# One megabyte of expert weights loaded before the router's table exists, and stores waited for one use later

## The reference

```python
x = x + gnn0(layernorm(x))    # h = x W_conv; sum of messages over edges; h W_lin + b_lin
x = x + ffn0(layernorm(x))    # a small 3-layer network on decoded features of each row
x = x + gnn1(layernorm(x))    # 3 times: relu(A (x W[l]) + b[l]), W[l] is 512x512
x = x + ffn1(layernorm(x))    # a tree of 15 tests picks one of 16 experts for each row
# expert e: gelu(x W1[e] + b1[e]) W2[e] + b2[e],  W1[e] 512x2048, W2[e] 2048x512, float32
```

## Time and profile before

| | us |
|---|---|
| median of 3 runs | 576.83 (575.34 to 577.37) |
| the profiled execution, its time | 578.86 |
| its span, first to last instruction | 577.1 |
| PE busy | 526.0 (91%) |
| DVE busy | 188.4 (33%) |
| ACT busy | 143.6 (25%) |
| POOL busy | 73.1 (13%) |
| mean granted TensorE clock | 0.978 of full |

### The profile page before, as it was taken

One profiled execution on the slowest core, in us unless ns is written; L12 is line 12 of the kernel. 1 busy time (PEld: TensorE's weight loads), 2 busy tenths in 40 slices (PEclk: granted clock), 3 DMA queues, 4 the chain that ended last, 5 costly groups with the idle time before them and its releaser, 6 DMA issues.

```text
span 577.1 us, 10036 instructions
## 1 busy us (share of the span) xinstructions
PE 526.0 (91%) x3215; PEld 286.8 (50%) x3215; DVE 188.4 (33%) x566; ACT 143.6 (25%) x504; POOL 73.1 (13%) x99
## 2 busy tenths in 40 slices
PE   1969999989999999999999599999999999978884
PEld 1536667544457466445455245555544364434332
DVE  5998999644410110256730100111111011100110
ACT  1547666112102011003122112222222042202211
POOL 4000000090000000000002222211211212122011
PEclk9979999979999999999999799999999999999998
DMA  6159930001120010027799999999999999999980
GB/s 128 14 174 429 429 133 19 18 1 53 39 73 2 0 73 0 7 86 229 288 389 418 413 396 424 420 424 423 422 423 419 419 430 412 421 416 433 420 371 21
DMA packets 26513, 145.84 MB, mean 253 GB/s; under 512 B 10479, under 2 KB 12729, under 8 KB 16882
## 3 DMA queue, kind: packets, MB, share of 16 engines
q1 hardware_dynamic: 23282, 142.92, 61.4%
q0 software_dynamic: 3200, 2.50, 2.1%
HBM read 142.38 MB, written 4.72 MB: 255 GB/s over the span
## 4 chain that ended last, share of the span: by engine, by line
PE 68%; DMA 16%; DVE 8%; issue 3%; ACT 2%; DVEq 1%; ACTq 1%; POOL 0%; POOLq 0%; SPq 0%
PE P L1168 14%; PE P L1082 13%; DMA w<-in_L_ffn_W 12%; PE P L955 9%; PE P L965 7%; PE P L789 6%; PE P L974 4%; DMA XT<-normed_rows,C 2%; PE P L1133 2%; DMA out<-XT,C 2%; DVE stats L1317 2%; DVE H L1292 1%; PE P L790 1%; PE P L1146 1%; PE P L869 1%
## 5 line engine op out<-in xcount | busy, mean ns | idle before, releaser
L1168 PE MATMUL P<-w,FB 128*64 128x256 f32 x1024 | 115.9, 383 | 2.2 <-DMA w<-in_L_ffn_W 2.2
L1082 PE MATMUL P<-w,H 128*64 128x512 f32 x448 | 100.0, 595 | 9.3 <-DMA w<-in_L_ffn_W 8.8
L1168 PEld LDWEIGHTS P<-w,FB 128*64 128x64 f32 x1024 | 72.1, 138 | 40.6 <-issue 6.6
L718 ACT ACTIVATE FB<-P,FB 128x64 f32<-128x64 f32 x256 | 54.4, 361 | 121.8 <-PE P L1133 121.8
L1575 DVE COPY H<-P 128x512 f32<-128x512 f32 x30 | 20.7, 692 | 195.5 <-PE P L1082 195.0
L789 PE MATMUL P<-H 125*126 125x500 bf16 x176 | 59.0, 414 | 8.1 <-DVE H L1292 4.7
L1082 PEld LDWEIGHTS P<-w,H 128*64 128x64 f32 x448 | 32.1, 137 | 68.7 <-issue 59.3
L1292 DVE TENSOR_SCALAR H<-iota,small 125x626 bf16<-125x626 f16 x176 | 56.6, 382 | 8.7 <-issue 6.9
L619 ACT ACTIVATE H<-G,small 125x126 bf16<-125x126 f16 x132 | 44.2, 392 | 35.3 <-PE P L790 21.8
L955 PE MATMUL P<-G,XT 128*125 128x512 f32 x120 | 52.0, 592 | 0.0
L965 PE MATMUL P<-C,H 125*128 125x313 f32 (+1 forms) x160 | 42.4, 425 | 0.0
(11 more groups left out here) (315 smaller groups left out, 441.8 us busy)
## 6 DMA issues: line engine op xcount, KB each, us to landing
w<-in_L_ffn_W SPq DMA_DIRECT2D x53, 2048.0 KB, 24.8
w<-in_L_ffn_W SPq DMA_DIRECT2D x14, 1024.0 KB, 9.6
G<-in_L_gnn_W SPq DMA_DIRECT2D x3, 1024.0 KB, 5.3
G<-in_L_ffn_W SPq DMA_DIRECT2D x2, 1024.0 KB, 8.3
C<-in_L_ffn_W SPq DMA_DIRECT2D x2, 1024.0 KB, 9.4
xs<-in_L_ffn_W SPq DMA_DIRECT2D x2, 1024.0 KB, 10.2
xn<-in_L_ffn_W SPq DMA_DIRECT2D x2, 1024.0 KB, 10.3
xs<-in_x SPq DMA_DIRECT2D x1, 1120.0 KB
```

The lines of the kernel that those rows point to most:

```text
L718: g = nc.scalar.activation(hT[:, m, :], P[:, 3 + rd, c * SA:(c + 1) * SA], ACT.Gelu, bias=bT[b][:, m:m + 1])
L1082: mm = nc.tensor.matmul(P[g * SA:(g + 1) * SA, h, :], xT[b][:, k, :], w1a[k][:, h, g], start=(k == 0), stop=(k == KD - 1))
L1168: mm = nc.tensor.matmul(P[g * SA:(g + 1) * SA, 7, 0:256], hT[:, m, :], w2_sb[b][:, m, g * 256:(g + 1) * 256], start=False, stop=(m == MH - 1))
```

## The change

- SP: after the block of tile 2's W1 that goes to xs, it waits until the router's last logits are out (`s_lgT` is 2) and loads the first quarter of tile 2's W2 to `XT[:, 0:2048]`. The later load of that quarter to `w2_sb[0]` is gone. PE's second layer of tile 2 takes quarter 0 from there.
- The small arrays leave that part of XT: `y_sb` to the last chunk of xs, `x_row` and `x_rowB` to the last chunk of xn, `y_sbB` to H, `sel` to the end of XT. DVE therefore waits for the stored norm rows ahead of the copy to `x_row`, and clears `x_rowB` after it, no longer behind the one-hot; ACT waits for the stored rows of x.
- POOL: a store is waited for when its `y_sb` buffer is used again, two tiles later. `s_yfree` is raised in `scatter`, after the next gather is issued.
- POOL starts its part of the second norm once `feat` is written. PE does one more `keep_warm` matmul between the feature transposes and the first layer of `ffn0`.

```diff
--- before.py
+++ after.py
@@ -183,11 +183,13 @@
         xTB = H[:, 2048:2048 + KD * SB_].rearrange("p (k s) -> p k s", k=KD)
         hT = FB[:, 0:MH * SA].rearrange("p (m s) -> p m s", m=MH)
         hTB = FB[:, MH * SA:MH * ROWS].rearrange("p (m s) -> p m s", m=MH)
-        y_sb = [XT[:, 1024 + b * 256:1280 + b * 256] for b in range(2)]
-        y_sbB = XT[:, 384:512]
-        sel = XT[:, 1792:1792 + NCH * SA].rearrange("p (c s) -> p c s", c=NCH)
-        x_row = XT[:, 0:256]
-        x_rowB = XT[0:2 * SB_, 512:768]
+        y_sb = [xs[:, NCH - 1, b * 256:(b + 1) * 256] for b in range(2)]
+        y_sbB = H[:, 2176:2304]
+        sel = XT[:, 2048:2048 + NCH * SA].rearrange("p (c s) -> p c s", c=NCH)
+        x_row = xn[:, NCH - 1, 0:256]
+        x_rowB = xn[0:2 * SB_, NCH - 1, 256:512]
+
+        w2_two = XT[:, 0:HID].rearrange("p (m n) -> p m n", m=4)
 
 
         maps = C[:, :, :].rearrange("p c n -> p (c n)")[:, HID:NCH * NPAD]
@@ -233,6 +235,7 @@
         s_edges, s_x, s_wconv, s_blin, s_cols = (sem(n) for n in ("edges_in", "x_in", "wconv_in", "blin_in", "cols_in"))
         s_wlin, s_ffnw, s_win, s_gw, s_bg2 = (sem(n) for n in ("wlin_in", "ffnw_in", "win_in", "gnnw_in", "bg2_in"))
         s_w1 = [[sem(f"w1_in{b}_{j}") for j in range(2)] for b in range(2)]
+        s_w2_two = sem("w2_in_tile2_quarter")
         s_w1_two, s_w2_end, s_w1q = sem("w1_in_tiles2_5"), sem("w2_in_end"), sem("tile0_w1_block_used")
         s_w2 = [[sem(f"w2_in{b}_{h}") for h in range(2)] for b in range(2)]
         s_iota, s_ident, s_rev, s_ones, s_loops, s_winz = (sem(n) for n in
@@ -374,6 +377,8 @@
             first_of_two(1)
             sp.wait_ge(s_ost, 16 * 2 * NCH)
             first_of_two(2)
+            sp.wait_ge(s_lgT, 2)
+            sp.dma_start(w2_two, W2[2, 0:HID // 2, :].rearrange("(p m) n -> p m n", p=128)[:, 0:4, :]).then_inc(s_w2_two, 16)
             sp.wait_ge(s_xst, 16 * 2 * NCH)
             sp.wait_ge(s_xrow, 1)
             first_of_two(3)
@@ -399,7 +404,7 @@
                 else:
                     sp.wait_ge(s_h, 4)
                 sp.dma_start(w1_sb[1][:, k, :], W1[bass.ds(e, 1), j * 256:(j + 1) * 256, :].rearrange("a (p r) n -> p (a r) n", r=2)[:, r, :]).then_inc(s_w1[1][j], 16)
-            for q in range(4):
+            for q in range(1, 4):
                 h, r = q // 2, q % 2
                 sp.wait_ge(s_l2, q + 1)
                 sp.dma_start(w2_sb[0][:, 4 * q:4 * q + 4, :],
@@ -500,6 +505,7 @@
             nc.gpsimd.memset(feat, 0.0).then_inc(s_fz, 1)
 
             pool.wait_ge(s_ahead, 1)
+            pool.wait_ge(s_feat, 1)
             for c in range(NCH):
                 nc.gpsimd.tensor_scalar(xn[0:NC, c, FCOLS:DIM], xs[0:NC, c, FCOLS:DIM], mv[0:NC, c, 0:1], rstd[0:NC, c:c + 1],
                                         ALU.subtract, ALU.mult).then_inc(s_ln, 1)
@@ -508,7 +514,7 @@
 
             pool.wait_ge(s_gh, NCH * 3)
             nc.gpsimd.memset(b2_rows, 0.0).then_inc(s_b2z, 1)
-            pool.sem_inc(s_yfree, 2)
+
             def hold(sem, value):
 
                 pool.wait_ge(sem, value)
@@ -525,8 +531,12 @@
                                              in_offset=bass.IndirectOffsetOnAxis(ap=row_in, axis=0),
                                              bounds_check=2 * N_NODES - 1, oob_is_err=False).then_inc(s_xr, 16)
 
-            def scatter(i, b, count):
-
+            def scatter(p, b, count):
+
+                i = 2 * p + b
+                if not (isinstance(p, int) and p == 0):
+                    hold(s_yst[b], 16 * p)
+                pool.sem_inc(s_yfree, 1)
                 pick(row_out[b], 0, i, count)
                 hold(s_ycp, i + 2)
                 nc.gpsimd.indirect_dma_start(out=out.rearrange("t (g n) -> (t g) n", g=2),
@@ -555,16 +565,15 @@
                 i = 2 * p + b
                 hold(s_xT, i + 2)
                 gather(i + 2, 2 * i + 3)
-                scatter(i, b, 2 * i + 4)
+                scatter(p, b, 2 * i + 4)
                 if isinstance(p, int) and i == LARGE:
                     pool.wait_ge(s_ycpB, 1)
                     nc.gpsimd.indirect_dma_start(out=out.rearrange("t (g n) -> (t g) n", g=4),
                                                  out_offset=bass.IndirectOffsetOnAxis(ap=row_outB, axis=0), in_=y_sbB, in_offset=None,
                                                  bounds_check=4 * N_NODES - 1, oob_is_err=False, compute_op=ALU.add).then_inc(s_ystB, 16)
-                hold(s_yst[b], 16 * p + 16)
-                pool.sem_inc(s_yfree, 1)
-
-            with pool.Fori(0, LARGE // 2) as p:
+            for b in range(2):
+                move_rows(0, b)
+            with pool.Fori(1, LARGE // 2) as p:
                 for b in range(2):
                     move_rows(p, b)
             for b in range(2):
@@ -573,7 +582,7 @@
                 for b in range(2):
                     move_rows(p, b)
             for b in range(2):
-                scatter(2 * last + b, b, 4 * last + 3 + b)
+                scatter(last, b, 4 * last + 3 + b)
             for b in range(2):
                 hold(s_yst[b], 16 * last + 16)
             pool.wait_ge(s_ystB, 16)
@@ -696,6 +705,7 @@
 
             nc.scalar.activation(rstd[0:1, 0:1], ones[0:1, 0:1], ACT.Gelu)
             act.sem_inc(s_ycp, 1)
+            act.wait_ge(s_ost, 16 * 2 * NCH)
             act.wait_ge(s_b1T, 1)
             nc.scalar.activation(b1T[:, :, 0:MH].rearrange("p e (q r) -> p e q r", r=8),
                                  P[:, 5, 0:256].rearrange("p (r e q) -> p e q r", r=8, q=2), ACT.Copy)
@@ -883,6 +893,7 @@
                     t = nc.tensor.matmul(P[g * GT:(g + 1) * GT, c // 4, (c % 4) * NC:(c % 4 + 1) * NC], feat[:, c, :],
                                          ident[0:NC, 0:NC], start=True, stop=True)
             t.then_inc(s_fT, 1)
+            keep_warm(1, C[0:NC, 0, 0:DIM])
             pe.wait_ge(s_fTc, 1)
             pe.wait_ge(s_win, 16 * 20)
             pe.wait_ge(s_wint, 1)
@@ -1155,17 +1166,21 @@
                     slot_tokens()
 
                 def second_a(q):
-                    if q % 2 == 0:
-                        if b or first:
+                    apart = isinstance(p, int) and i == 2
+                    if apart and q == 0:
+                        pe.wait_ge(s_w2_two, 16)
+                    elif q % 2 == 0 or (apart and q == 1):
+                        if b or first or q < 2:
                             pe.wait_ge(s_w2[b][q // 2], 16 * (p + 1))
                         else:
-                            pe.wait_ge(s_w2[0][q // 2], 16 * (p + 2))
+                            pe.wait_ge(s_w2[0][1], 16 * (p + 2))
                     elif end and q == 3:
                         pe.wait_ge(s_w2_end, 16)
                     pe.wait_ge(s_gelu, 4 * i + q + 1)
                     for m in range(4 * q, 4 * q + 4):
                         for g in range(2):
-                            mm = nc.tensor.matmul(P[g * SA:(g + 1) * SA, 7, 0:256], hT[:, m, :], w2_sb[b][:, m, g * 256:(g + 1) * 256],
+                            w2 = w2_two[:, m] if apart and q == 0 else w2_sb[b][:, m]
+                            mm = nc.tensor.matmul(P[g * SA:(g + 1) * SA, 7, 0:256], hT[:, m, :], w2[:, g * 256:(g + 1) * 256],
                                                   start=False, stop=(m == MH - 1))
                     if not more:
                         mm.then_inc(s_l2, 1)
@@ -1454,7 +1469,6 @@
                     link(tt(right[:, :, :, 1], level[d][0:NC], here, ALU.mult))
                     link(tt(right[:, :, :, 0], level[d][0:NC], right[:, :, :, 1], ALU.subtract))
             nc.vector.tensor_copy(oh16[0:NC], leaf[0:NC]).then_inc(s_oh, 1)
-            nc.vector.memset(x_rowB, 0.0).then_inc(s_rowB, 1)
 
             cnt16, top, big, cap, jump, extra = (sv(230 + 16 * i, NE) for i in (3, 4, 5, 6, 7, 8))
             cmp, val, le = sv(374, NE, MORE), sv(518, NCH, NE), keys
@@ -1490,8 +1504,10 @@
                 nc.vector.tensor_copy(xT[b].rearrange("p (g j) s -> p j g s", g=2),
                                       P[:, 6, 256:512].rearrange("p (j g s) -> p j g s", j=2, g=2)).then_inc(s_xTc, 1)
 
+            dve.wait_ge(s_xst, 16 * 2 * NCH)
             dve.wait_ge(s_xrow, 1)
             nc.vector.tensor_copy(x_row, P[:, 0, 0:256]).then_inc(s_xrowc, 1)
+            nc.vector.memset(x_rowB, 0.0).then_inc(s_rowB, 1)
             link(stt(jump[0:NC, :], cnt16[0:NC, :], float(NE * ROWS // SA), extra[0:NC, :], ALU.add, ALU.subtract))
             link(stt(jump[0:NC, :], jump[0:NC, :], float(SA), cap[0:NC, :], ALU.mult, ALU.subtract))
             link(tt(jump[0:NC, :], jump[0:NC, :], home[0:NC, :], ALU.subtract))
```

## The result

The kernel after takes 571.97 us in the median of 20 runs (569.98 to 574.96), the kernel before 575.70 us in 20 runs beside it (573.65 to 578.91): 0.9936 of the time, interval 0.9920 to 0.9951, so 3.7 us less. The sum of the prediction was 6.9 us and its forecast 570.2. The profiled execution after took 572.42 us, with a span of 569.6.

A forecast was written before the change was run, and what follows sets the result against it. The prediction took the expert stage's weight stream plus a fixed 20.3 us chain to bound the kernel, with everything ahead of it counting in full. Terms 2.5 + 0.8 + 3.2 + 0.5 - 0.1 = 6.9 us gave 570.2 us, range 567.8 to 574.0.

The forecast's parts named there:

- The bound: Expert stage: the program ends 20.3 us after the last W1 half lands, so the stream of weights sets the end.
- The 6: Last tiles: PE's waits for weights grow from 11.0 us by about 6, as PE time saved in tile 2 is lost again.
- The first network's clock: ffn0, 121 to 128 us: filling PE's 1.07 us gap with a keep_warm avoids half clock and saves 3.2 us.
- it may be that the fastest had no drop of the clock: Clock in ffn0: from the fastest run only the other 3.7 us come off, giving 571.6; forecast set at 570.2.
- One reason given for the remaining gaps being harmless: PE's remaining gaps in ffn0: the last tiles keep their clock although PE waits 1.2 us at a time there.
- POOL behind the features: First network: starting POOL's norm after DVE's features stops tiny DVE operations being drawn out, saving 0.5 us, between 0 and 0.77.
- The expert stage: Expert-stage terms: quarter of W2 2.5 us, stores 0.8 us, less 0.1 us lost to small moves of arrays.
- the stores: POOL in the expert stage: waiting for stores later lets tile 3's gather start earlier, saving 0.8 us, between 0 and 1.5.
- the moved quarter: Router's end: a quarter of tile 2's W2 fills the stream's hole from 277 us, saving 2.5 us, or 0 if it doesn't fit.
- the dip at 335 to 340 us: Weight stream after tile 2's stall: 356 GB/s instead of 421 as SP's W2 load comes late, costing 0.77 us.
- The stall goes: PE in tile 2: its 6.23 us wait for tile 3's rows vanishes, the gather starting at about 314.7 and landing at 321.
- The bounds 568.0 and 572.0: Whole kernel: limits of the 570.2 us forecast under its own bounds, in the case given 0.55.

The follow-up runs named there:

- experiment 1: Kernel before with only the two first-network edits, POOL's wait for the features and one more keep_warm: 574.27 us, ratio 0.9969 to the kernel before.
- experiment 3: Kernel before with only one first-network edit each: POOL's wait for the features 574.63 us (0.9967), the added keep_warm 575.03 us (0.9969).
- experiment 7: Kernel after with the first quarter of tile 2's W2 loaded at its old place, none to XT: 573.53 us, 0.9953 of the kernel before.
- experiment 8: Kernel after with POOL waiting right behind each store as before, measured twice: 574.55 us (0.9975) and 574.80 us (0.9979 of the kernel before).
- experiment 2: Kernel before with only the expert-stage edits, without the two first-network edits: 572.88 us, 0.9944 of the kernel before.
- Experiment 9: Kernel after with tile 3's gather issued ahead of tile 0's store and s_yfree raised for both tiles up front: 572.23 us, 0.9928 of before.

## Why the prediction was right in kind and wrong in size

**Trace against trace** the sum comes out: the span went from 577.1 to 569.6 us, 7.5 less, where 6.9 were forecast. That is luck in the choice of execution, as the next paragraphs show. Between the medians it is 3.7, a little over half of the sum.

**The bound** was read rightly. The stream sets the end, and the last 20 us are the same. PE's waits for weights did not grow by 6 us, though, but by 0.5 (11.5 against 11.0). The 6 was inconsistent by the prediction's own terms: a stream that ends 3.3 us earlier takes 3.3 of the 6.2 saved. Measured, PE's stall is 4.1 us shorter and the second stretch, the stream's, 3.7 (285.92 to 282.18), which leaves 0.4.

**The first network's clock, 3.2 us: this term failed.** Its size was right for the one execution that it was read from: 3.28 us by the table, where 3.2 were forecast. What failed is "I take 3.2 us" as a saving in every execution. The fall is not a property of the program. In three traces with both gaps unfilled it lasted 6.8, 3.4 and 0 us. The kernel before loses 1.8 - 0.6 = 1.2 us to it on average (experiment 1 less POOL's wait), with an interval as wide as that of the ratio, 0.3 to 2.1. The granted clock agrees: over the executions of experiment 1 its mean is 0.9839, of the kernel before beside them 0.9817, which is 2.5 us less at half clock and by the rate of the table some 1.2 us, an estimate. The same for POOL's wait alone and the keep_warm alone gives 0.8 and 0.3 us. The text saw the case, "it may be that the fastest had no drop of the clock", and let it shift the forecast by 0.3 us only, from 569.9 to 570.2. The trace of before also was one of the longest executions, 578.86 us against medians of 575.70, 575.26 and 575.6 to 576.5 in the other sets of runs.

**The keep_warm** was taken as the cause of the full clock, and it was not needed for it. With POOL's wait in place and no keep_warm the clock stayed full in both traces, and six executions of after without it are as fast as those with it. Whether the keep_warm would do it alone is open: it has one trace with a full clock and 1.8 us in time. Whether two smaller gaps or one filled one matter more for the chance of a fall, these few traces can't settle. What they settle is that the filler shortens nothing by more than 0.06 us where the clock is full anyway. One reason given for the remaining gaps being harmless doesn't hold in each trace: that the clock stays full in the last tiles, where PE waits for weights. In five of the 14 traces it falls to half for 3.4 us near 500 to 510 us, four times around such a wait of 2.7 us or so and once behind one of 2.07. PE waits for weights there anyway, so this costs nothing that the second stretch shows.

**POOL behind the features, 0.5 us:** measured 0.55, with the filler 0.61.

**The expert stage, 2.5 + 0.8 - 0.1 = 3.2 us:** measured 3.2 on the kernel before (2.2 to 4.2), and some 2.3 on top of the first network's edits. The sum is right, in part by luck, since its two terms are not independent and neither has its forecast size alone. With the stores as before, the moved quarter brings nothing (574.6 and 574.8 us against 574.3 and 574.6 in experiments 1 and 3). With the quarter at its old place, the new stores bring some 0.9 (573.53 against 574.4). Together they bring 2.3 (some 572.1). Each of these medians is uncertain by half a microsecond to one. Clear of that is only that the old stores cost the new kernel 2 to 3 us, twice; the rest of the pattern is argued from the windows of experiments 7 and 8. The quarter brings forward the time at which the queue of loads runs dry, and the stall of PE holds back the release of the buffers that fills it again. The prediction worked out the dip at 335 to 340 us for the fuller queue of before, and from an execution with a small dip. So the stores came out too small (0.8 us, where 2 to 3 are lost without them). The quarter came out too large: alone it brings nothing that can be told from none, since what it gives at the hole is lost at the dip, and 0.7 us of it goes again at 307 to 328 us in any case.

**"The stall goes":** only from 6.23 to 2.11 us. The gather was issued earlier than forecast, 310.96 and not 314.7. But 2.7 us behind the store it took 10.2 us instead of 6.2; 7.4 us behind it, in experiment 2, it took 6.3 and the stall was gone. Experiment 9 shows that the rest is worth nothing.

**The level:** the forecast was 570.2, and it became 571.97, the upper side of the range. The bounds 568.0 and 572.0, given for the case that every term holds, don't follow from the terms: at their largest these add up to 8.2 us, at their smallest without a fall of the clock to 5.4, so 568.7 to 571.4, and the measured time lies past that. The kernel before is at 575.70 in 20 runs rather than 576.83 in 3, and 3.7 us come off.

## What to carry to other kernels

- A clock that falls after gaps of a microsecond may fall in one execution and not in the next. Before a lowered clock is put into a sum, look at a second trace, or weigh it with the chance; the gap that mattered here was shortened at its source, POOL beside small operations of DVE, and no filler was needed then.
- Two edits around one queue must be costed together: ask when it runs dry and when it is refilled, after both. Here the edit that brings the first forward was worth nothing measurable until the second came forward too.
- A dip read from one execution is a sample. The landing of one store moved it between 0.7 and 5.0 us in the same program.
- Count the waits of a stage from its first instruction to its last. A fixed cut at 500 us dropped one here when the kernel got faster, and turned a small rise into a fall.

## What the runs showed of the hardware

- PE's clock went to half after idle stretches of 0.7 to 0.8 and 1.07 us, with 1.27 us of 32-column transposes between. It lasted 6.8, 3.4 or 0 us in three traces, and 6.8 us in one where the first of the gaps was 3.28 us. At half clock this part, nearly all of it PE's, loses 1.58 us per 3.4 us.
- PE's clock also fell around its wait for rows in tile 2: for 3.4 us in the three traces where the wait was 1.9 to 2.1 us, for 6.8 or 10.2 us in the eight where it was 3.0 to 7.0, and not at all in the three without the wait.
- A DVE operation on 125x20 takes 0.51 us beside POOL's norm and 0.18 without it. Of those on 125x5 beside it, some take 0.38 to 0.48 us and others 0.17, as without it.
- A gather of 128 rows lands in about 6.2 us by itself, in 10.1 to 11.6 us when issued 2.7 us behind an adding store (four traces), in 6.3 and 6.5 us when issued 7.4 us behind it (two), and the store itself in 8.3 or 11.8 us in two executions of the same program.
